# Every gather of the edge stream waits for the sum of the step 17 places in front of it

## What is computed

```
edge_index = stack([src, dst])
x = x + gnn(layernorm(x), edge_index, W, b)   # mean of the source rows of each node, concat, @ W.T + b
x = x + ffn(layernorm(x), ...)                # 8 experts, the best 2 of each node, GELU between two products
msg_sum = segment_sum(h[src], dst)
agg = msg_sum / maximum(deg, 1)
```

## Time and profile before

| what | us |
|---|---|
| median of three timed executions | 1795.77 |
| lowest and highest of them | 1793.36, 1799.16 |
| span of the profiled execution | 1787.5 |
| PE busy in it | 1241.8 (69%) |
| VectorE (DVE) busy | 812.6 (45%) |
| POOL busy | 948.0 (53%) |
| gathers of line 662, POOL busy | 681.0 + 59.6 |

### The profile page before, as it was taken

How to read it: one execution, slowest core, us unless ns; L and a number is a source line. 1 busy time by engine, 2 the same in 40 slices (tenths; PEclk the granted TensorE clock), 3 DMA queues, 4 the chain that set the end, 5 groups by cost and what they waited for, 6 DMA issues and landing times.

```text
span 1787.5 us, 23229 instructions
## 1 busy us (share of the span) xinstructions
PE 1241.8 (69%) x5751; PEld 942.1 (53%) x5751; DVE 812.6 (45%) x2587; ACT 463.2 (26%) x1019; POOL 948.0 (53%) x995
## 2 busy tenths in 40 slices
PE   3223777765874778678787688688788868795881
PEld 2101343442652556556566566566666656684771
DVE  8312663452444445344434444445366565642333
ACT  4200000210220134124124224233322413463440
POOL 3574035666556655655655655665556565115544
PEclk9855998777886889898888889888889889997886
DMA  9732044433333333343333333343344333324553
GB/s 335 247 104 64 1 153 151 133 99 100 110 99 94 107 111 106 115 121 95 113 111 101 110 112 104 109 122 101 115 128 120 105 109 107 101 78 132 160 159 119
DMA packets 128488, 212.63 MB, mean 119 GB/s; under 512 B 25378, under 2 KB 94295, under 8 KB 128119
## 3 DMA queue, kind: packets, MB, share of 16 engines
q0 software_dynamic: 48352, 129.18, 25.2%
q1 hardware_dynamic: 77561, 81.17, 13.7%
q10 hardware_dynamic: 2446, 0.80, 0.2%
HBM read 167.37 MB, written 50.87 MB: 122 GB/s over the span
## 4 chain that ended last, share of the span: by engine, by line
PE 44%; another core or an unknown queue 17%; issue 16%; DVE 11%; ACT 6%; DVEq 2%; DMA 2%; POOL 1%; ACTq 0%; POOLq 0%
PE psum L764 16%; PE psum L833 9%; PE psum L858 8%; DVE acc L1125 5%; PE psum L777 4%; ACT expert_buf L633 2%; PE psum L812 2%; PE psum L778 1%; ACT expert_buf L625 1%; PE psum L845 1%; ACT region L570 1%; DVEq L1118 1%; PE psum L806 1%; PE psum L789 1%
## 5 line engine op out<-in xcount | busy, mean ns | idle before, releaser
L662 POOL DMA_INDIRECT work<-h_rows,srcs x719 | 681.0, 947 | 576.3 <-PE psum L764 324.0
L1125 DVE TENSOR_TENSOR acc<-acc,psum 128x257 f32 x830 | 350.3, 422 | 713.5 <-PE psum L764 329.1
L764 PE MATMUL psum<-work 128*128 128x257 f32 x1438 | 483.6, 450 | 193.7 <-DVE acc L1125 121.9
L764 PEld LDWEIGHTS psum<-work 128*128 128x128 f32 x1438 | 274.7, 219 | 300.3 <-issue 279.1
L833 PE MATMUL psum<-expert_buf 128*128 128x128 f32 x1792 | 235.3, 288 | 40.5 <-ACT expert_buf L625 34.3
L833 PEld LDWEIGHTS psum<-expert_buf 128*128 128x128 f32 x1792 | 230.3, 203 | 50.4 <-ACT expert_buf L625 36.7
L858 PE MATMUL psum<-region,expert_buf 128*128 x896 | 244.7, 422 | 11.6 <-issue 6.5
L633 ACT ACTIVATE expert_buf<-psum,b_col 128x128 f32<-128x128 f32 x448 | 127.8, 370 | 429.7 <-remote 220.0
L858 PEld LDWEIGHTS psum<-region,expert_buf 128*128 128x128 f32 x896 | 186.2, 216 | 49.9 <-issue 21.6
L764 PE MATMUL psum<-region,work 128*128 (+1 forms) x222 | 81.2, 486 | 106.0 <-issue 67.0
L999 DVE TENSOR_TENSOR work<-psum,rel 128x1152 f32<-128x1152 f32 x98 | 126.3, 1289 | 53.6 <-issue 36.7
(11 more groups left out here) (248 smaller groups left out, 896.3 us busy)
## 6 DMA issues: line engine op xcount, KB each, us to landing
expert_buf<-queue SPq DMA_DIRECT2D x112, 128.0 KB
answers<-expert_buf SPq DMA_DIRECT2D x112, 128.0 KB
work<-h_rows,srcs POOLq DMA_INDIRECT x719
region<-in_L_ffn_W_dram SPq DMA_DIRECT2D x16, 512.0 KB
h_rows<-region SPq DMA_DIRECT2D x7, 896.0 KB
own<-h_rows SPq DMA_DIRECT2D x49, 128.0 KB
own<-x_rows SPq DMA_DIRECT2D x49, 128.0 KB
out_dram<-acc SPq DMA_DIRECT2D x49, 128.0 KB
```

Of the source, the lines that this page charges most:

```text
L662: pool.indirect_dma_start(place_of(g)[:, 0:D], None, h_rows, bass.IndirectOffsetOnAxis(srcs[:, cell_of:cell_of + 1], 0)).then_inc(got[g % ...
L764: summed.up(pe.matmul(STEP_BANKS[t % BANKS][:, 0:GW], hot[:, k, :], rows, start=True, stop=True))
L1125: added.up(dve.tensor_tensor(sums, sums, STEP_BANKS[t % BANKS][:, 0:GW], ALU.add))
```

## The change

The wait for the sum of step t - 17 is taken out of its condition and now stands in front of each gather:

```
             if g is not None:
                 if g >= RING:
                     pool.wait_ge(got[g % RING], 16 * (g // RING))
-                if g >= SHARED + EXTRA + RING:
-                    summed.wait(pool, t - RING)
+                summed.wait(pool, t - RING)
                 cell_of = CELLS + g if g < SHARED else t
                 pool.indirect_dma_start(place_of(g)[:, 0:D], None, h_rows,
```

## The result

The changed kernel takes 1734.7 us (median of four, 1728.8 to 1739.7) against 1797.5 us for the kernel before (median of four, 1793.4 to 1799.3): a ratio of 0.966, 95% interval 0.963 to 0.970. The forecast was 1741 us in a range of 1715 to 1776. The profiled span went from 1787.5 to 1731.9 us, 55.6 us less.

The account below looks back on a forecast made before the run. The prediction took early steps to be bound by late news of sums, a cost of gathers issued without a pause. Terms -70 + 8.6 + 7 = -54.5 us gave span 1733; with 8.3 us for timed runs, 1741 us, range 1715 to 1776.

Parts of the forecast that it names:

- What bounds the kernel: Early steps: gathers issued without a pause make news of finished sums late; the adder idles 72.1 us in 15 waits.
- the crawl: Early steps beside unheld gathers, 73.3 to 159.5 us: 17 adds in 86.2 us, 5.07 us per step.
- feedback: POOL's wait for a sum: a late sum stops the gathers, which ends the lateness; the first 80 gathers lack it.
- News that a sum is done: Claim that in early steps this arrives late, while the gathers those steps need were issued long before.
- Steps 5 to 95: Early stretch, one gather per two steps: 157.1 us to 87 us, 12 us of it lateness; saving 70 us.
- Steps 96 to 111: Each step now wants its own gather beside it: 12.5 us becomes 21 us, +8.6, plus 7 us for slow steps returning.
- a return of the crawl: Around steps 79 to 111, while POOL makes up 6 missing gathers, slow steps come back: 7 us lost, bounds 0 and 15.
- From step 112 on: Order, waits and lead of 17 as before; cost nothing, with a spread of some 5 us.
- The sum: All terms over the profiled span: -70 + 8.6 + 7 = -54.5 us, giving a span of 1733 us.
- Held pace: Rival, 20%: early steps run at 1.32 us each, as where gathers were already held; 28 us saved, 1767 us.
- the crawl is not of the gathers: Rival, 5%: something else makes early sums late, slow steps stay 86 us long; 1804 to 1811 us.
- the lead was worth its price: Rival, 5%: without it steps 5 to 111 run at 1.84 us each, 27 us slower, 1823 us.

Follow-up runs that it names:

- late jobs: Four of the five measuring jobs, those in which the unchanged kernel before took 1788 to 1798 us and sums came late.
- prompt job: The one job, with the first four follow-up kernels, in which the unchanged kernel before took 1429 us and no sums came late.
- the spaced run: Kernel before without added waits, POOL clearing an idle buffer behind each of the first 80 gathers: 1744.5 us, ratio 0.973; earlier 1464.0 us, ratio 1.024.
- the two parts of the change that ran: Kernel before plus the wait at gathers 9 to 47 alone (1437.8 us, ratio 1.006), or from gather 48 on (1438.7 us, ratio 1.008).
- with 34 steps: Kernel before, with its first 80 gathers waiting for the sum 34 steps in front rather than 17: 1429.0 us, ratio 1.000.

## Why the prediction was right

*What bounds the kernel.* Confirmed in the late jobs: the crawl comes with gathers issued without a pause, and ends 10 to 12 us after the last of them, wherever that lies. What I called feedback is only one way to get there: the spaced run has none, and no late sum in its first 95 steps. And the lateness is not in the program alone, which no row of the one trace could tell: the prompt job has the same rate and none of it.

One reading of the rows was wrong: 5 us is not how late a sum is. The idle time in front of an add starts at the add before it, and three steps are under way at once (three PSUM banks). The pair that runs from 75.19 to 75.89 us is that of step 8, and the add of step 8 is not the one at 79.42 but this:

```profile
89.23 0.42 DVE L1125 TENSOR_TENSOR acc<-acc,psum 128x257 f32 x1 [4.49 <-remote]
```

It comes 13.3 us behind the record of its matmuls. The trace has a record of the sum's signal too, at 89.10 us. For steps 10 to 22 the distance is 14.2 to 15.6 us, and a third of it is the 5 us per step. It stays so until the gathers stop. The last two that come far too late are those of steps 23 and 24: their matmuls run at about 158 and 163 us, their adds at 171.1 and 171.8 us. "News that a sum is done" stays my reading: the profile models the ends of matmuls. For it speaks that the matmuls of steps 9 and 10 had started, at 80 and 85 us, before the signal of step 8 came.

*Steps 5 to 95.* Forecast 157 to 87 us, a saving of 70 with 12 us of late sums in it. Measured 157.1 to 80.5, with 3.9 us of late sums. The saving was undersized by 7 us: I took late sums at the density of the earlier trace rows, and here hardly any occur. That those stretches have the routing and the experts beside the stream is the difference that I can name; it was not tested.

*Steps 96 to 111.* Forecast +8.6 for the pace and +7 for a return of the crawl. Measured +10.3. The crawl did return, from step 100 on (six late sums, 11.1 us), but it was short: POOL ran into its wait at 167 us, and at 172 us the late sums were over. No add came more than 10.0 us behind its matmuls, against 15.6 in the crawl.

*From step 112 on.* This step failed: "Cost nothing". It cost 8.9 us up to step 149 and 1.8 behind it. I let the price of the lost lead end at step 111, where the kernel before also falls back to 17 gathers. But the lead is spent over the steps behind it. In the prompt job, without late sums, a kernel held from gather 48 on loses nothing up to step 111 and 9.1 us from there to step 149, since POOL runs at its bound of 1.25 us. In the changed kernel five late sums (18.8 us) stand in the stretch, against six (13.3 us) in that of the kernel before, so the 8.9 us are a mixture, whose parts these runs don't separate. The second pair of traces (the late job of the change and the kernel before again) has the terms at -77.6, +13.1, +6.0 and +1.5 us: the same signs, with some 3 us of play between one stretch and the next.

*The sum.* -54.5 forecast, -55.6 measured in the span: terms missed by -7, -5 and +11 us, which cancel. That the sum is right to 1 us is luck; each term by itself was off by more. The median is 6 us under the forecast, since the runs lie 3 us above the profiled span here rather than 8.

*The rivals.* Held pace (1767 us) falls: the early steps took 0.88 us each. That the crawl is not of the gathers falls by the run with the wait from gather 48 on, which moved its end by 39 us. The Trainium skill's rule of "SBUF — State Buffer", "Who interferes with whom", had stood on that side. The prompt job agrees with what it says: there the same gathers slow neither matmuls nor adds (93 adds in 75.0 us beside 61 gathers). It does not follow that POOL's gathers cannot delay a step: in the late jobs they do, up to 15.6 us from a matmul's record to its add. That the lead was worth its price is wrong in the late jobs. In the prompt one, where no late sum is to be avoided, the two parts of the change that ran lose 0.6 and 0.8%; in the traces this comes from POOL's pace at steps 112 to 149, not by the 1.84 us per step of this rival.

## What to carry to other kernels

Work that one engine does far ahead need not be free; here it cost 3% in the late jobs. When an engine runs hundreds of us in front of its use while another's waits end by something the profile cannot name, try to bound the lead by a wait that is needed later anyway. Here it cost no work on another engine, and its price was the first stretch in which that lead would have been spent. Price that stretch to the point where the stream has caught up, not to the point where the old lead ended. When steps overlap, measure how late a signal is from the record of its own matmul, not from the idle time in front of the add: here 15 us, not 5. And run the kernel before beside every experiment: here the same program took 1429 us or 1790 us, and parts of this edit cost time in the one case and save it in the other.

## What the runs showed that was not expected

The same program took 1429 us in one job and 1788 to 1798 in four others, with the same busy times to within 1% on DVE, ACT and POOL. The kernel with the wait from gather 48 on was traced in both kinds: spans 1437.4 and 1772.4 us, DVE busy 813.0 us in both, PE busy 1148.9 and 1243.2 us at a granted clock of 0.92 and 0.84. PE's 94 us are the smaller part of the 335 us; the rest stands in waits. The longest of the changed kernel that end by a releaser the profile does not know:

```profile
ACT expert_buf L633 <- remote: 235.7, 25, 17.1
...
DVE acc L1124 <- remote: 228.1, 68, 9.8
...
POOL work L661 <- remote: 103.8, 48, 3.4
ACT pair_t L584 <- remote: 61.5, 9, 16.1
ACT expert_buf L625 <- remote: 51.0, 7, 16.2
DVE expert_buf L1182 <- remote: 49.5, 7, 16.7
```

By the program each of these instructions waits for a signal of PE (some of them for another too), on three engines (hidden products at lines 633 and 625, sums at 1124 and 661, transposes at 584, results at 1182). In the prompt job not one wait of the kernels with the wait from gather 48 on or with 34 steps ends by "remote", on any engine. The late traces also lack records that the prompt ones have. The signal of the sums is recorded 704 times for 830 steps in the kernel before, and 827 times in the prompt trace of the kernel with the wait from gather 48 on; and in no late trace does the profile give the gathers a time from issue to landing, where the prompt ones have 2.8 us. First the kernel before, then the prompt trace:

```profile
region<-h_rows,srcs POOLq DMA_INDIRECT x63
```
```profile
region<-h_rows,srcs POOLq DMA_INDIRECT x63, 2.8
```

So counts of waits by "remote" are rough in late traces; idle times themselves are not touched by it. What delays these signals, and what makes a job prompt or late, these runs leave open.

The rate at which gathers make sums late lies between 1.74 us (none of 92 sums in the first steps) and 1.25 us apart (a crawl of 5 us per step); at 1.58 us on average there was one with a lead of 17 steps. With a lead of 10 steps there was none, at the same average (47 gathers in 74.3 us, and 47 in 76.9 us in the kernel with 10 steps at the start only) and with the same 1.25 us inside a run of gathers. So the length of a run without a pause may count beside the mean rate; no run was made to tell the two apart. And the lateness outlasts its cause: the last sums came late 10 to 12 us after the last gather had been issued, with a DMA share of 0.04.
